# Head sums of a twelve-head attention over two streams instead of three: tiles 0 and 1 added before TensorE

## The chip, the core and the metric

One core of one Trainium2 chip runs the whole program. The metric is the time of one execution on the device, in microseconds (us). Three timed runs of the kernel before took 866.79, 868.4 and 868.53 us; their median is 868.4 us.

## The reference

The input `x` has 32 images of 384 channels and 32x32 = 1024 positions. Each image is normalised over 32 groups of channels, projected, passed through an attention that has no query and key but only statistics of one projection, projected again, and added to the input:

```python
w = einsum('bnc,oc->bno', gn(x), qkv_w)            # 12 heads of d = 32
norm = sqrt(sum(w * w, over positions))            # per channel
s = sum((w / max(norm, 1e-12))**2, over d)         # one score per head and position
Pi = softmax(s * temp, over the 12 heads)
Pi_n = Pi / (sum(Pi, over positions) + 1e-8)
dots = einsum('bhn,bhnd->bhd', Pi_n, w * w)
out = -(w * Pi) / (1 + dots)
y = x + einsum('bnc,oc->bno', out, out_w) + out_b
```

Everything is fp32. The score of a head is a sum over its 32 channels of `w * w`, each weighted by the channel's inverse squared norm and the head's `temp`.

## The kernel before

Channels lie on the 128 partitions in three tiles of [128, 1024] (t = 0, 1, 2), positions on the free axis; `W` of an image is written to the three PSUM tiles `acc[:, t]`. Each tile holds four heads; its 128 output channels are ordered so that the head is the fast index, and `PIB[:, t]` (the softmax weights of four heads, spread over 128 partitions through DRAM) matches that order.

Both projections are made in split fp32: each operand is a high part (`W1H`, `XH`, `W2H`, `UH`, rounded for the fast mode of TensorE) and a low remainder (`W1L`, `XL`, ...). A product of one output tile is 18 matmuls of 128x512: for each k of three, high by high and high by low weight (`n` = 0, 1), then the low operand (`n` = 2), each in two halves of 512 positions.

Images are software-pipelined, and the order on every engine is written out by hand as a function `step(i)`; steps 2 to 31 follow a prologue, and the loop over images 2 to 29 is unrolled four times. Engines meet at counting semaphores only. In step i:

- TensorE (PE) makes the first product of image i (three tiles, lines 824 to 826), then the second product of image i-1 (lines 827 to 830). Within tile 0 of the second product, before its first low term, `head_sums(i)` (line 789) runs: for each of three tiles and each quarter of the positions a matmul of the squares with `headsum[:, t]` (128x32), summed in `scores`. In the last step with an image (i = 31, `late`), they stand two matmuls earlier.
- ScalarE (ACT) squares each tile of `acc` into `WS` with a sum per channel into `sumsq` (`square_w`, line 501), copies `acc` into `WV` (`keep_w`, line 512), rounds the weighted `WV` of image i-1 to `UH` (`u_hi`, line 491), and makes `XN` and `XH` of image i+1 (lines 519, 529).
- VectorE (DVE) adds bias and input to the finished tiles (`finish`, line 1149), then, for image i-1, `dot` for three tiles (line 1041), four small steps of `attention`, `weigh` for three tiles (line 1067), and `u_lo`: `UL = WV - UH` (line 1141, two tiles before the group statistics, one after). `head_sum_weights(i)` (lines 990 to 996) makes `inv` and `headsum` from `sumsq` of all three tiles; softmax follows (lines 1005 to 1033).
- GpSimd (POOL) only makes `XL = XN - XH` for image i+1 (`x_lo`, line 424).
- SyncE (SP) loads, stores, and in `spread_pi` (line 366) writes `PIT` to DRAM in three DMAs and reads it back, broadcast, as three DMAs of 528 KB into `PIB`.

The prologue (image 0) and image 31 use other forms (`attend_tile`, `product_by_k`, heads of tile 0 spread by TensorE).

Of the kernel before, what the change touches and what calls it, by code (L numbers as in the profile page):

```python
# [33 lines left out]
P = 128  # L34
# [12 lines left out]
HEADSUM_STEPS = 3  # L47
IDLE_TURNS = (4, 4)
SM_SHIFTED, SM_STEPS = 3, 8
ATTENDED = 3 + 4  # L50
# [33 lines left out]
def conv_attention(nc, x, qkv_w, temp, out_w, out_b, y):  # L84
# [5 lines left out]
    HPT = P // D  # L90
    HALVES = N // BANK
# [8 lines left out]
    with ExitStack() as ctx:  # L100
# [46 lines left out]
        inv = sb("inv", [P, 2, T])  # L147
# [5 lines left out]
        pi_part = sb("pi_part", [P, HPT])  # L153
        pi_heads = sb("pi_heads", [P, BLOCKS, HPT])
        PIT = sb("PIT", [P, T, QUAD + 1])
        PIB = sb("PIB", [P, T, BLOCKS * QUADS, QUAD + 1])
# [13 lines left out]
        small = spread_ps[:, 0]  # L170
        temp_ps = scores[:, C:C + HEADS]
# [32 lines left out]
        headsum_step = sem("headsum_step")  # L204
        scores_done = sem("scores_done")
# [3 lines left out]
        pi_spread = [sem(f"pi_spread_{t}") for t in range(T)]  # L209
# [52 lines left out]
        def rows_moved(j, t, more=0):  # L262

            return j.counts(16, more - (16 if t == 0 and True else 0))
# [75 lines left out]
        def _(sp):  # L340
# [25 lines left out]
            def spread_pi(j):  # L366

                if has(j):
# [3 lines left out]
                    tiles = range(1 if by_pe(j) else 0, T)  # L372
                    for t in tiles:
                        rows = pi_dram[t * HPT:(t + 1) * HPT].rearrange("h (b q n) -> q (h b) n", b=BLOCKS, q=QUADS)
                        sp.dma_start(rows, PIT[:, t, :]).then_inc(pi_written[t], 16)
                    for t in tiles:
                        sp.wait_ge(pi_written[t], rows_moved(j, t, 16))
                        heads = pi_dram[t * HPT:(t + 1) * HPT].unsqueeze(0)\
                            .to_broadcast([D, HPT, BLOCKS * QUADS * (QUAD + 1)])
                        sp.dma_start(PIB[:, t].rearrange("p b n -> p (b n)"), heads).then_inc(pi_spread[t], 16)  # L380

# [26 lines left out]
        def _(pool):  # L408
# [7 lines left out]
            pool.tensor_copy(mixed_w2.rearrange("p (m d h) -> p m d h", d=D, h=HPT),  # L416
                             raw_w2.rearrange("p (m h d) -> p m d h", d=D, h=HPT)).then_inc(w2_mixed, 1)
# [8 lines left out]

            def step(i):
                for t in range(T):
                    x_lo(i + 1, t)
# [23 lines left out]
        def _(act):  # L453
# [83 lines left out]
            def widen_heads(j):  # L537

                act.wait_ge(heads_kept, pe_spread(j))
                if j.follows(1):  # L540
                    act.wait_ge(u_step, (j - 1).counts(U_STEPS, 1))
                act.activation(wide_heads(j).rearrange("p (b d h) -> p b d h", b=BLOCKS, d=D),
                               pi_heads[:].unsqueeze(2).to_broadcast([P, BLOCKS, D, HPT]), ACT.Copy)\
# [62 lines left out]
            def x_hi_first():  # L606
# [20 lines left out]
            act.activation(wide_part(last).rearrange("p (d h) -> p d h", d=D),  # L627
                           pi_part[:].unsqueeze(1).to_broadcast([P, D, HPT]), ACT.Copy).then_inc(heads_widened, 1)
# [14 lines left out]
        def _(pe):  # L643
            def turn_weights(ks):
# [3 lines left out]
                for k in ks:  # L648
                    for m in range(T):
                        raw = columns1[:, k, m, :] if k < T else columns2[:, k - T, m, :]  # L650
                        if k < T:
                            into = turned(k)[:, m * P:(m + 1) * P].rearrange("p (d h) -> p h d", h=HPT)
# [45 lines left out]
            def first_product(i, t):  # L698
# [6 lines left out]
                if has(i):  # L705
                    acc_left(i - 2, t)
                    product(acc[:, t, :], t, (W1H, W1L), (XH, XL), before, {}).then_inc(m1_done, 1)

# [80 lines left out]
            def head_sums(i):  # L789
# [7 lines left out]
                for t in range(T):  # L797
                    for q in range(QUADS):
                        block_q = square_tile(i, t).rearrange("p (b q r) -> p q b r", q=QUADS, r=QUAD)[:, q]
                        last = pe.matmul(scores[q * QUAD:(q + 1) * QUAD, 0:N // QUADS], headsum[:, t, :],  # L800
                                         block_q, start=(t == 0), stop=(t == T - 1))
# [17 lines left out]
            def step(i):  # L819
# [7 lines left out]
                second_product(i - 1, 0, {(1, 2) if late else (2, 0): lambda: head_sums(i)})  # L827

# [448 lines left out]
```

## Time and profile before

| what | before |
|---|---|
| timed runs | 866.79, 868.4, 868.53 us |
| profiled execution, first to last instruction | span 864.9 us |
| around the span (timed runs less span) | 1.9 to 3.6 us |
| PE busy | 851.6 us, 98% |
| DVE busy | 750.2 us, 87% |
| ACT busy | 528.3 us, 61% |
| POOL busy | 232.6 us, 27% |
| granted TensorE clock | 1.00 of full speed |

The profile is of one execution apart from the timed runs; its whole time is not given, only the span. Busy times are unions per engine. A line of the page's groups holds the line in the kernel, the engine, the operation, output and inputs, their shapes and count; then busy us and mean ns of one; then idle us in front of it and what ended them.

### The profile page before, as it was taken

What the parts mean: (1) busy time and instruction counts of PE and PEld (TensorE: products, weight loads), DVE (VectorE), ACT (ScalarE), POOL (GpSimd) and SP (SyncE); (2) the same over time, 40 slices, a digit from 0 to 9 for tenths busy, and PEclk for the clock granted to TensorE, in tenths of its full rate; (3) what the DMA queues carried; (4) which work ended last, traced back from release to release, by engine and by line L of the source; (5) the groups of instructions that cost most, each with busy time, mean ns of one, the idle gap of its engine ahead of it and who ended that gap; (6) DMA issues with size and microseconds to landing.
All of it is one profiled execution on the core that took longest, in us unless ns stands there. A gap on an engine that the chain in (4) does not pass through costs nothing.

```text
span 864.9 us, 14022 instructions
## 1 busy us (share of the span) xinstructions
PE 851.6 (98%) x4290; PEld 677.7 (78%) x4290; DVE 750.2 (87%) x1396; ACT 528.3 (61%) x680; POOL 232.6 (27%) x106
## 2 busy tenths in 40 slices
PE   7999999999999999999999999999999999999997
PEld 6767788777787777787777787777887777887776
DVE  7989889898888888888888898888898888898777
ACT  3567656567555677556676556676565675566642
POOL 2432123332123331133331233321233321233300
PEclk9999999999999999999999999999999999999999
DMA  7324665544664544664535654445655446645225
GB/s 279 119 79 153 225 229 185 185 148 169 225 227 161 197 146 181 226 223 160 180 150 198 228 213 168 163 145 220 227 186 196 141 163 225 228 175 186 88 86 197
DMA packets 45259, 157.42 MB, mean 182 GB/s; under 512 B 19866, under 2 KB 23962, under 8 KB 37274
## 3 DMA queue, kind: packets, MB, share of 16 engines
q1 hardware_dynamic: 36856, 154.10, 48.5%
q10 hardware_dynamic: 8354, 2.85, 1.3%
q14 instruction: 40, 0.33, 0.1%
q8 instruction: 9, 0.15, 0.1%
HBM read 104.47 MB, written 52.45 MB: 181 GB/s over the span
## 4 chain that ended last, share of the span: by engine, by line
PE 92%; DVE 4%; issue 1%; DMA 1%; ACT 1%; DVEq 0%; ACTq 0%
PE acc L678 86%; PE spread_ps L800 5%; DVE stats L906 1%; DVE WS L1041 1%; DMA PIB<-pi 0%; DMA X<-in_x 0%; DVE WV L1101 0%; DVE X L1149 0%; PE acc L655 0%; DVE WS L1080 0%; ACT WS L501 0%; DMA pi<-PIT 0%; DVE X L1116 0%; ACT WV L512 0%; PE spread_ps L815 0%
## 5 line engine op out<-in xcount | busy, mean ns | idle before, releaser
L424 POOL TENSOR_TENSOR XL<-XN,XH 128x1024 fp32r<-128x1024 f32 x93 | 222.9, 2414 | 571.7 <-ACT XH L529 548.2
L501 ACT ACTIVATE WS<-acc 128x1024 f32<-128x1024 f32 x96 | 98.4, 1026 | 240.5 <-PE acc L678 197.1
L678 PE MATMUL acc<-XH,W1H 128*128 128x512 f32 x574 | 177.3, 390 | 0.1
L678 PE MATMUL acc<-XH,W1L 128*128 128x512 f32 x574 | 176.8, 389 | 0.0
L678 PE MATMUL acc<-UH,W2H 128*128 128x512 f32 x558 | 172.6, 390 | 1.3 <-ACT WV L512 1.2
L678 PE MATMUL acc<-UH,W2L 128*128 128x512 f32 x558 | 172.3, 390 | 0.0
L678 PE MATMUL acc<-XL,W1H 128*128 128x512 f32 x576 | 146.2, 389 | 0.0
L678 PE MATMUL acc<-UL,W2H 128*128 128x512 f32 x558 | 145.3, 396 | 0.0
L1149 DVE SCALAR_TENSOR_TENSOR X<-acc,bias,X 128x1024 f32<-128x1024 f32 x93 | 116.3, 1276 | 31.0 <-PE acc L678 31.0
L678 PEld LDWEIGHTS acc<-UL,W2H 128*128 128x128 f32 x558 | 102.3, 188 | 32.2 <-issue 11.9
L678 PEld LDWEIGHTS acc<-XL,W1H 128*128 128x128 f32 x576 | 108.0, 188 | 22.7 <-POOL XL L434 0.3
L678 PEld LDWEIGHTS acc<-XH,W1L 128*128 128x128 f32 x574 | 107.7, 188 | 22.5
L678 PEld LDWEIGHTS acc<-XH,W1H 128*128 128x128 f32 x574 | 107.3, 188 | 23.0 <-issue 0.9
L678 PEld LDWEIGHTS acc<-UH,W2H 128*128 128x128 f32 x558 | 104.3, 188 | 24.9 <-issue 2.1
L1041 DVE CUSTOM_DVE_ANT_0 WS<-PIB,WS 128x1024 f32<-128x1024 f32 x94 | 113.5, 1222 | 10.2 <-DMA PIB<-pi 8.1
L906 DVE BATCH_NORM_STATS2 stats<-X 128x6 f32<-128x512 f32 x192 | 120.0, 680 | 2.5 <-DMA X<-in_x 2.5
L678 PEld LDWEIGHTS acc<-UH,W2L 128*128 128x128 f32 x558 | 104.6, 188 | 22.4 <-issue 0.4
L491 ACT ACTIVATE UH<-WV 128x1024 fp32r<-128x1024 f32 x93 | 95.0, 1054 | 41.7 <-DVE WV L1067 37.5
L519 ACT ACTIVATE XN<-X,norm 128x1024 f32<-128x1024 f32 x91 | 112.3, 1235 | 0.4 <-DVE XN L961 0.4
L1141 DVE TENSOR_TENSOR UL<-WV,UH 128x1024 fp32r<-128x1024 f32 x93 | 111.2, 1222 | 0.1
L1067 DVE SCALAR_TENSOR_TENSOR WV<-WV,dots,PIB 128x1024 f32<-128x1024 f32 x90 | 110.3, 1281 | 1.1
L529 ACT ACTIVATE XH<-X,norm 128x1024 fp32r<-128x1024 f32 x90 | 111.0, 1233 | 0.0
(119 smaller groups left out, 501.3 us busy)
## 6 DMA issues: line engine op xcount, KB each, us to landing
PIB<-pi SPq DMA_DIRECT2D x94, 528.0 KB, 5.1
X<-in_x SPq DMA_DIRECT2D x31, 1536.0 KB, 6.3
out_y<-X SPq DMA_DIRECT2D x30, 1536.0 KB, 6.5
gathered<-stats_rows ACTq DMA_DIRECT2D x28, 72.0 KB, 5.1
pi<-PIT SPq DMA_DIRECT2D x94, 16.5 KB
X<-in_x SPq DMA_DIRECT2D x3, 512.0 KB, 4.7
out_y<-X SPq DMA_DIRECT2D x1, 1024.0 KB, 6.0
out_y<-X SPq DMA_DIRECT2D x2, 512.0 KB, 2.6
```

Source lines behind the costliest of these rows:

```text
L424: pool.tensor_tensor(XL[:, t, :], XN[:, t, :], XH[:, t, :].bitcast(F32), ALU.subtract).then_inc(xl_done, 1)
L491: act.activation(u_tiles(j)[0][:, t, :], w_tile(j, t), ACT.Copy).then_inc(uh_done, 1)
L501: act.activation(square_tile(i, t), acc[:, t, :], ACT.Square, accum_out=sumsq[:, t:t + 1]).then_inc(squared, 1)
L519: act.activation(XN[:, t, :], x_tile(j, t), ACT.Identity, bias=shift_j, scale=rstd_j).then_inc(xn_done, 1)
L529: act.activation(XH[:, t, :], x_tile(j, t), ACT.Identity, bias=shift_j, scale=rstd_j).then_inc(xh_done, 1)
L678: last = pe.matmul(out[:, h * BANK:(h + 1) * BANK], w[:, k, m * P:(m + 1) * P], r[:, k, h * BANK:(h + 1) * BANK], start=(n == 0 and k == 0 ...
L800: last = pe.matmul(scores[q * QUAD:(q + 1) * QUAD, 0:N // QUADS], headsum[:, t, :], block_q, start=(t == 0), stop=(t == T - 1))
L906: last = dve.bn_stats(stats[:, k, :], X[:, j.slot, k * BANK:(k + 1) * BANK])
L1041: dve.tensor_tensor_reduce(in_blocks(square_tile(j, t)), PIB[:, t, :, 0:QUAD], in_blocks(square_tile(j, t)), 1.0, 0.0, ALU.mult, ALU.add, ...
L1067: dve.scalar_tensor_tensor(in_blocks(w_tile(j, t)), in_blocks(w_tile(j, t)), dots[:, 3, t:t + 1], PIB[:, t, :, 0:QUAD], ALU.mult, ALU.mult ...
L1141: dve.tensor_tensor(low[:, t, :], w_tile(j, t), high[:, t, :].bitcast(F32), ALU.subtract).then_inc(ul_done[t], 1)
L1149: dve.scalar_tensor_tensor(x_tile(j, t), acc[:, t, :], bias[:, t:t + 1], x_tile(j, t), ALU.add, ALU.add).then_inc(y_done, 1)
```

## The change

Tiles 0 and 1 get a common layout of eight heads by sixteen channels per head and tile, tile 2 keeps four heads by thirty-two. The channels of w that belong to one head of the first eight now lie half in tile 0 and half in tile 1, on the same partitions. So the squares of both tiles, each scaled by the channel's inverse squared norm, can be added elementwise, and one matmul stream with the constant `head_temp` serves both. From image 2 on:

- DVE: `pair_weight(i, t)` makes the inverse squared norms of tiles 0 and 1 as soon as each is squared; `head_sum_weights` handles tile 2 only, with its inverse in PSUM; `u_lo` leaves the engine.
- ACT: `scale_square` scales the squares of tile 0 (after `keep_w(i, 0)`) and of tile 1 (after the last `u_hi`).
- POOL: `u_lo` of tile 0, the addition of the scaled squares, `u_lo` of tiles 1 and 2, then `x_lo`.
- PE: `head_sums` has two streams; of the second product the high terms of tile 0 come first, then the head sums, the high terms of tile 1, the low terms of tiles 0 and 1, and tile 2. The late step keeps its order.
- `PIB` has two bands instead of three tiles: three writes to DRAM, then two broadcast reads of 528 KB. Images 0 and 31 write all three parts too.

```diff
+        paired = sb("paired", [P, 2, N])
-        PIB = sb("PIB", [P, T, BLOCKS * QUADS, QUAD + 1])
+        PIB = sb("PIB", [P, BANDS, BLOCKS * QUADS, QUAD + 1])
+        inv_ps = small[:, QUAD:QUAD + 2 * T].rearrange("p (s t) -> p s t", t=T)
...
 # SyncE, spread_pi
+                    for band, of_band in enumerate(BAND_HEADS):
+                        for t in range(of_band.start // HPT, of_band.stop // HPT):
+                            sp.wait_ge(pi_written[t], j.counts(16, 16))
...
 # GpSimd
+            def u_lo(j, t):
+                pool.wait_ge(uh_done, j.counts(T, t + 1))
+                wait_weighed(pool, j, T - 1)
+                pool.wait_ge(m2_done, j.counts(T))
+                pool.tensor_tensor(UL[:, t, :], w_tile(j, t), UH[:, t, :].bitcast(F32),
+                                   ALU.subtract).then_inc(ul_done[t], 1)
             def step(i):
+                if i.follows(2) and has(i):
+                    u_lo(i - 1, 0)
+                    pool.wait_ge(pair_step, i.counts(PAIR_STEPS, 2 - PAIR_STEPS * PAIRED))
+                    pool.tensor_tensor(paired[:, 0, :], paired[:, 0, :], paired[:, 1, :], ALU.add).then_inc(pair_step, 1)
+                    u_lo(i - 1, 1)
+                    u_lo(i - 1, 2)
                 for t in range(T):
                     x_lo(i + 1, t)
...
 # ScalarE
+            def scale_square(i, t):
+                if has(i):
+                    act.wait_ge(headsum_step, i.counts(HEADSUM_STEPS, 2 * t + 2))
+                    act.wait_ge(squared, i.counts(T, t + 1))
+                    act.wait_ge(scores_done, i.counts(1))
+                    act.activation(paired[:, t, :], square_tile(i, t), ACT.Copy, scale=inv[:, 1, t:t + 1]).then_inc(pair_step, 1)
             def step(i):
                 square_w(i, 0)
                 keep_w(i, 0)
+                scale_square(i, 0)
                 u_hi(i - 1, 0)
                 square_w(i, 1)
                 u_hi(i - 1, 1)
                 u_hi(i - 1, 2)
+                scale_square(i, 1)
                 square_w(i, 2)
...
 # TensorE, head_sums
+                if paired_sums(i):
+                    pe.wait_ge(pair_step, i.counts(PAIR_STEPS, PAIR_STEPS - PAIR_STEPS * PAIRED))
+                    streams = [(head_temp[:, 0, :], paired[:, 0, :]), (headsum[:, T - 1, :], square_tile(i, T - 1))]
 # TensorE, step
+                second_high(i - 1, 0)
+                head_sums(i)
+                second_high(i - 1, 1)
+                second_low(i - 1, 0)
+                second_low(i - 1, 1)
+                second_high(i - 1, 2)
+                second_low(i - 1, 2)
...
 # VectorE
+            def pair_weight(j, t):
+                link = chain(headsum_step, j.counts(HEADSUM_STEPS, 2 * t))
+                dve.wait_ge(squared, j.counts(T, t + 1))
+                dve.wait_ge(scores_done, j.counts(1))
+                link(dve.tensor_scalar(inv[:, 0, t:t + 1], sumsq[:, t:t + 1], NORM_FLOOR ** 2, None, ALU.max))
+                link(dve.reciprocal(inv[:, 1, t:t + 1], inv[:, 0, t:t + 1]), follows=False)
 # attention, step 0: two sums in place of one
+                    dve.tensor_reduce(total[:, 0:2], PIB[:, 0, :, QUAD].unsqueeze(1).to_broadcast([P, 2, BLOCKS * QUADS]),
+                                      AX_X, ALU.add).then_inc(u_step, 1)
+                    done = dve.tensor_reduce(total[:, 2:3], PIB[:, 1, :, QUAD], AX_X, ALU.add)
             def step(i):
+                pair_weight(i, 0)
                 weigh(i - 1, 0)
                 weigh(i - 1, 1)
                 weigh(i - 1, 2)
-                u_lo(i - 1, 0)
-                u_lo(i - 1, 1)
+                pair_weight(i, 1)
                 group_moments(i + 1)
                 head_sum_weights(i)
                 group_norm(i + 1)
-                u_lo(i - 1, 2)
                 group_stats(i + 2, [0])
                 softmax_shift(i)
```

## Rows read from the trace of the kernel before

**Rows 1.** The page's first part: TensorE's busy time, share of the span, instructions.
```profile
PE 851.6 (98%) x4290; PEld 677.7 (78%) x4290; DVE 750.2 (87%) x1396; ACT 528.3 (61%) x680; POOL 232.6 (27%) x106
```
**Rows 2.** Chain that ended last, one step of 28: start, us, what.
```profile
416.72 1.43 PE spread_ps L800 x24
418.15 24.72 PE acc L678 x108
```
**Rows 3.** Timeline of TensorE, one step: start, us, engine, line, operation.
```profile
401.60 0.62 PE L678 MATMUL acc<-XH,W1H 128*128 128x512 f32 x2
...
413.84 0.62 PE L678 MATMUL acc<-UH,W2H 128*128 128x512 f32 x2
...
427.75 0.62 PE L678 MATMUL acc<-XH,W1H 128*128 128x512 f32 x2
```
**Rows 4.** Timeline of VectorE and ScalarE, same step; in brackets idle time before.
```profile
404.19 1.23 DVE L1041 CUSTOM_DVE_ANT_0 WS<-PIB,WS 128x1024 f32<-128x1024 f32 x1
...
405.59 1.23 DVE L1041 CUSTOM_DVE_ANT_0 WS<-PIB,WS 128x1024 f32<-128x1024 f32 x1 [0.17 <-DMA PIB<-pi]
...
407.71 3.68 DVE L1067 SCALAR_TENSOR_TENSOR WV<-WV,dots,PIB 128x1024 f32<-128x1024 f32 x3
...
409.03 1.06 ACT L491 ACTIVATE UH<-WV 128x1024 fp32r<-128x1024 f32 x1 [0.96 <-DVE WV L1067]
...
410.11 1.03 ACT L501 ACTIVATE WS<-acc 128x1024 f32<-128x1024 f32 x1
...
411.13 2.00 ACT L491 ACTIVATE UH<-WV 128x1024 fp32r<-128x1024 f32 x2
...
414.19 1.03 ACT L501 ACTIVATE WS<-acc 128x1024 f32<-128x1024 f32 x1 [1.07 <-PE acc L678]
...
415.34 0.17 DVE L990 TENSOR_SCALAR inv<-sumsq 128x3 f32<-128x3 f32 x1 [0.96 <-ACT WS L501]
```
**Rows 5.** Page, DMA issues: count, KB each, us to landing.
```profile
PIB<-pi SPq DMA_DIRECT2D x94, 528.0 KB, 5.1
```
**Rows 6.** Timeline of ScalarE and GpSimd: waking after an XH; three subtractions in a row.
```profile
418.62 1.24 ACT L529 ACTIVATE XH<-X,norm 128x1024 fp32r<-128x1024 f32 x1
...
419.99 2.40 POOL L424 TENSOR_TENSOR XL<-XN,XH 128x1024 fp32r<-128x1024 f32 x1 [18.28 <-ACT XH L529]
...
812.09 7.20 POOL L424 TENSOR_TENSOR XL<-XN,XH 128x1024 fp32r<-128x1024 f32 x3 [18.08 <-ACT XH L529]
```
**Rows 7.** Groups by shape: busy us, mean ns of one, idle before.
```profile
L491 ACT ACTIVATE UH<-WV 128x1024 fp32r<-128x1024 f32 x93 | 95.0, 1054 | 41.7 <-DVE WV L1067 37.5 <-DVE WV L1101 4.2
...
L519 ACT ACTIVATE XN<-X,norm 128x1024 f32<-128x1024 f32 x91 | 112.3, 1235 | 0.4 <-DVE XN L961 0.4
...
L450 POOL TENSOR_TENSOR X<-XN,X 128x512 f32<-128x512 f32 x1 | 1.3, 1273 | 40.6 <-ACT XN L637 40.6
```
**Rows 8.** Timeline near the end: ScalarE ends, TensorE resumes after a wait.
```profile
852.18 1.06 ACT L491 ACTIVATE XH<-WV 128x1024 fp32r<-128x1024 f32 x1 [2.11 <-DVE WV L1101]
...
853.29 0.72 PE L678 MATMUL acc<-XH,W2H 128*128 128x512 f32 x2
853.85 0.63 PE L678 MATMUL acc<-XH,W2L 128*128 128x512 f32 x2
```
**Rows 9.** Timeline of the first step with two streams (69 to 88 us) and the late one.
```profile
69.28 3.68 DVE L1067 SCALAR_TENSOR_TENSOR WV<-WV,dots,PIB 128x1024 f32<-128x1024 f32 x3
...
87.76 0.61 PE L678 MATMUL acc<-XH,W1H 128*128 128x512 f32 x2
...
820.05 0.61 PE L678 MATMUL acc<-XH,W1H 128*128 128x512 f32 x2
...
836.65 1.55 PE L678 MATMUL acc<-UL,W2H 128*128 128x512 f32 x6
```
**Rows 10.** Timeline of the prologue: a small VectorE instruction beside a GpSimd subtraction.
```profile
21.70 2.97 POOL L438 TENSOR_TENSOR W2L<-WV,W2H 128x384 fp32r<-128x384 f32 x3
...
23.96 0.27 DVE L924 TENSOR_SCALAR spread<-offset,part_mv 128x1 f32<-128x1 f32 x1
```

More of the change, by code:

```diff
@@ L260, in pe_spread, with band_rows, paired_sums @@
             return 2 if j.follows(1) else 1
-        def rows_moved(j, t, more=0):
-            return j.counts(16, more - (16 if t == 0 and True else 0))
+        def band_rows(t):
+            return PIB[:, BAND[t], :, 0:QUAD]
+        def paired_sums(j):
+            return j.follows(PAIRED)
         def tile_steps(j, t, steps):
@@ L651, in turn_weights @@
                         if k < T:
-                            into = turned(k)[:, m * P:(m + 1) * P].rearrange("p (d h) -> p h d", h=HPT)
+                            band = BAND_HEADS[m * HPT // PAIR_HEADS]
+                            heads = slice(m * HPT - band.start, (m + 1) * HPT - band.start)
+                            into = turned(k)[:, band.start * D:band.stop * D].rearrange("p (d h) -> p h d", h=len(band))[:, heads]
                         else:
@@ L707, in first_product, with second_high, second_low @@
                     product(acc[:, t, :], t, (W1H, W1L), (XH, XL), before, {}).then_inc(m1_done, 1)
+            def second_high(j, t):
+                pe.wait_ge(squared, (j + 1).counts(T, t + 1))
+                pe.wait_ge(w_kept, (j + 1).counts(T, t + 1))
+                for k in range(T):
+                    if t == 0:
+                        pe.wait_ge(uh_done, j.counts(T, k + 1))
+                    for n in (0, 1):
+                        term(acc[:, t, :], t, (W2H, W2L), (UH, UL), n, k)
+            def second_low(j, t):
+                for k in range(T):
+                    if t == 0:
+                        pe.wait_ge(ul_done[k], j.counts(1, 1))
+                    last = term(acc[:, t, :], t, (W2H, W2L), (UH, UL), 2, k)
+                last.then_inc(m2_done, 1)
             def second_product(j, t, inside):
@@ L987, in head_sum_weights @@
                     return
-                link = chain(headsum_step, j.counts(HEADSUM_STEPS))
+                tiles = slice(T - 1, T) if paired_sums(j) else slice(0, T)
+                done = 4 if paired_sums(j) else 0
+                link = chain(headsum_step, j.counts(HEADSUM_STEPS, done))
                 dve.wait_ge(squared, j.counts(T, T))
-                link(dve.tensor_scalar(inv[:, 0, :], sumsq[:], NORM_FLOOR ** 2, None, ALU.max))
-                link(dve.reciprocal(inv[:, 1, :], inv[:, 0, :]))
+                link(dve.tensor_scalar(inv_ps[:, 0, tiles], sumsq[:, tiles], NORM_FLOOR ** 2, None, ALU.max))
+                link(dve.reciprocal(inv_ps[:, 1, tiles], inv_ps[:, 0, tiles]))
                 if j.follows(1):
@@ L995, in head_sum_weights @@
                     dve.wait_ge(temp_kept, 3)
-                link(dve.tensor_tensor(headsum[:], head_temp[:],
-                                       inv[:, 1, :].unsqueeze(2).to_broadcast([P, T, QUAD]), ALU.mult), follows=False)
+                weights = headsum[:, tiles, :]
+                dve.tensor_tensor(weights, head_temp[:, tiles, :], inv_ps[:, 1, tiles].unsqueeze(2).to_broadcast(weights.shape),
+                                  ALU.mult).then_inc(headsum_step, HEADSUM_STEPS - 2 - done)
+            def pair_weight(j, t):
+                if not has(j):
+                    return
+                link = chain(headsum_step, j.counts(HEADSUM_STEPS, 2 * t))
[3 more added lines that the diff above has]
+                link(dve.reciprocal(inv[:, 1, t:t + 1], inv[:, 0, t:t + 1]), follows=False)
             def softmax_shift(j):
@@ L1029, in softmax_divide @@
                     for t in range(T):
-                        if j.follows(2) or rows_moved(j, t) > 0:
-                            dve.wait_ge(pi_written[t], rows_moved(j, t))
+                        dve.wait_ge(pi_written[t], j.counts(16))
                 link(dve.transpose(PIT[:, :, 0:QUAD], scores[:, P:P + HEADS * BLOCKS]))
```

106 lines of the change are left out of this document (58 added, 48 removed).

## The prediction

> **What bounds the kernel now.** I read the busy shares first: TensorE is busy for 851.6 of 864.9 us, all other engines have idle time [rows 1]. The chain of waits agrees: step after step it is TensorE alone, 24.72 us of product matmuls and 1.43 us of head sums, together 26.15 us [rows 2]. The timeline gives the same period: step 3 begins at 87.76 and step 31 at 820.05, so 28 steps take 732.29 us, 26.15 each [rows 9]. What a step of TensorE loses is thus worth 28 times as much, but only as long as no other engine's chain becomes longer than the step. The reader should see in the timeline of one step how near that is: ScalarE's third square waited 1.07 us for TensorE [rows 4], and GpSimd was idle for some 18 us of each step before its first subtraction [rows 6]. So the question is whether the new work fits into these gaps in its order, not whether the engines have the time in total.
>
> All times below are those of the step that begins at 401.60 [rows 3]. Its 54 matmuls up to 413.84 give one per 0.2267 us [rows 3]. The sum is made as a difference to the profiled execution (span 864.9 us) and then put on the median, 868.4 us; what lies around the span, 1.9 to 3.6 us, I leave as it is.
>
> **Part 1, what goes.** One of three streams of head sums leaves TensorE: 1.43/3 = 0.48 us [rows 2]. If nothing else changed, a step would take 25.67 us. Bounds: 0 (if the passes were limited by something other than the streamed columns) to 0.48. I take 0.48. Three `u_lo` leave VectorE, which was no bound; and one of three broadcasts of 528 KB goes [rows 5]. The third `dot` waited for one, 405.59 instead of a start some 0.2 us earlier [rows 4]. I take that wait as gone, since softmax also comes no later than before and less is moved; if it stays, 0.2 us come back below.
>
> **Part 2, the new chain.** The head sums now need both scaled squares and their sum, and the low terms of tile 0 need three `UL` that GpSimd makes around this sum. I follow the chain.
>
> VectorE: before `weigh` there are three small instructions more (the second sum of `attention`, two of `pair_weight`). None is longer than 0.20 us, the size of L990 with its gap [rows 4]; the independent ones overlap with their neighbours. I take 0.33 us in all, bounds 0.2 and 0.6. `weigh` moves from 407.71 to 407.71 - 0.21 + 0.33 = 407.83. `u_hi` of tile 0 followed `weigh` by 1.32 us [rows 4], now 409.15. The scaling of the first square fits in front of it: ScalarE was idle there for 0.96 us [rows 4] and the scaling takes about as long. The square of tile 1 started at 410.11, when TensorE had finished that tile (36 matmuls of 0.2267 = 8.16 us after 401.60, and the wake); it stays there within 0.06 us.
>
> ScalarE: two `u_hi` from 411.13 take 2.00 us; as two of 1.054 [rows 7] in 2.00 [rows 4] overlap by 0.11, the next one begins at 413.02. That is the second scaling. No row has a copy with one factor per partition. A plain copy from SBUF takes 1.054, one with factor and offset per partition 1.235 [rows 7]; I take the middle, 1.14. It ends at 414.16, and the third square, at 414.19 [rows 4], is just not delayed. So ScalarE's old gap hides it; if the cover were 0.1 us shorter, that would move the third square, on which nothing here hangs, as the path now goes through GpSimd.
>
> GpSimd: `u_lo` of tile 0 follows the third `weigh` (407.83 + 3.68 = 411.51 [rows 4]) and takes 2.41, done by 414.05. The addition wakes 0.13 us after ScalarE's end, as the subtraction at 419.99 did after 418.62 + 1.24 [rows 6]: 414.29. Three operations in a row take 7.20 us [rows 6]. For the addition, fp32 out, the nearest row is 1.273 us for half the size [rows 7]; doubled, 2.55, is its upper bound, as the fixed part counts twice, and 2.40 like the subtraction is my value. The sum is there at 414.29 + 2.40 = 416.69, the third `UL` at 421.49.
>
> TensorE: it is ready for the head sums at 416.65 [rows 2], so their wait costs 0.1 to 0.2 us. Then 0.95 us of head sums, 12 high and 4 low matmuls take it to about 421.4 without that wait (25.67 - 26 x 0.2267 = 19.78 after 401.60: 421.38). The third `UL` comes at 421.49; TensorE resumes 0.05 us after a release and its first pair takes 0.11 us more than a pair in stream (852.18 + 1.06 to 853.29; 0.56 to the next pair instead of 0.453) [rows 8]. So the low terms of k = 2 count from 421.65, and the last 26 matmuls end 5.89 us later, at 427.54 instead of 427.75 [rows 3]. **A step gains 0.21 us, not 0.48**, and its bound is now the chain through GpSimd; the first wait of head sums is inside it. 28 steps: -5.9 us.
>
> **Part 3, the two ends.** In step 2 VectorE was late: `weigh` began at 69.28, and the next step at 87.76 [rows 9]. No `dot` waited there, so `weigh` moves by 0.33 to 69.61, and the chain from it to the next step is 427.54 - 407.83 = 19.71 us: 89.32, 1.6 us later than before. In step 31 the order is the old one: only 14 matmuls stand between TensorE's beginning of the head sums and the low term of k = 2, while GpSimd needs two `u_lo` of 2.40 after the addition. That term began at 836.65 + 4 x 0.2267 = 837.56; now at 820.05 + 20.05 = 840.10 [rows 9]. What follows, the spreading of the last image's heads and its tail, hangs on TensorE's order behind it, so 2.5 us come on. Bounds for both ends together: 0 (if the tail has slack that I don't see) to 4.1; I take 4.1. The prologue's changes (one more 16.5 KB write, two copies of the weights instead of one, eight heads instead of four in two small products) I cost at nothing, 0.5 us if a `dot` there waits.
>
> **Sum.** -5.9 + 1.6 + 2.5 = -1.8: 866.6 us. A measurement of this kernel tells about 0.2%, 1.7 us, from no change, so the forecast lies at the edge of that.
>
> **Rivals.** (A) TensorE stays the bound. If GpSimd's chain were 0.27 us shorter, the step is 25.67: -13.4 us, and the ends +3.5: 858.5. For it: the scaling could cost the plain 1.054, the DVE chain could be quicker by the whole `dot` wait. Against: each of these gives 0.1. Times between 858.5 and 864 belong here.
>
> (B) The chain is dearer: scaling 1.235 (+0.10) and addition 2.55 (+0.15) make the step 26.19: +1.1, ends +4.6: 874. Slower from the point where the step passes 26.0 us, because then the ends are no longer paid for. With 0.6 us for VectorE's small instructions, another 0.3 us a step, over 880. For it: each of the values has a row at that end. Against: they would have to be dear together.
>
> (C) VectorE and GpSimd block each other. At 411.5 `pair_weight` of tile 1 (a maximum, then a reciprocal that follows 0.2 us later) meets the start of `u_lo` of tile 0. If the reciprocal had to stay behind the subtraction until 414.0, the second scaling would begin 1.2 us late, and so would all behind it: 28 x (1.2 - 0.2) and ends of 6.6: about 903. It decides if the reciprocal starts after GpSimd. Against it: in the prologue a one-element instruction of VectorE ran at 23.96 in 0.27 us within GpSimd's subtractions from 21.70 to 24.67 [rows 10], so it did not sit one out. The Trainium skill ("SBUF — State Buffer", section "SBUF: two separate sides") says that VectorE and GpSimd share a pair of ports as an exclusive lock for a whole instruction, taken by VectorE's operations in a two-port mode or with two SBUF inputs. By that rule the reciprocal could be locked out, and `dot` and `weigh` would have to keep clear of GpSimd's subtractions; the row at 23.96 shows no such wait for one element, and no run here shows the two-input case.
>
> (D) The head sums do not shrink (the four quarters share the array, and no row shows two streams): the step stays at 26.15 and the ends cost about 4: 872.
>
> **Chances.** Forecast 0.53, with times from 863.8 (gain 0.31 a step) to 869.4 (0.11), half of it on either side of 866.7: 0.26 faster, 0.27 same. A 0.19, faster. B 0.15, C 0.08, D 0.05, slower. Together 0.45 faster, 0.27 same, 0.28 slower. Range 860 to 875: it leaves out the best of A, the worst of B, and C. The likeliest case alone: 863.8 to 869.4.
>
> **What would show it.** In the timeline after: a step of 25.9 us; head sums of 0.95 us; TensorE idle for one or two tenths in front of the head sums and again before the low term of k = 2 of tile 0, released by GpSimd's `UL`; the chain of waits running through GpSimd and ScalarE instead of TensorE alone; the second scaling at 11.4 us into a step and 1.14 us long; 2.5 us of waiting in the late step. TensorE without idle and a step of 25.67 would be A; a reciprocal of `pair_weight` that starts when a subtraction ends would be C; head sums of 1.43 us, D. The forecast is wrong if the step is under 25.8 or over 26.1 us.

## The result, and the profile after

| | before | after |
|---|---|---|
| timed runs, median | 868.13 us (7, 866.79 to 869.46) | 870.62 us (7, 868.5 to 874.07) |
| ratio after / before, 95% interval | | 1.0037 [1.0026, 1.0047] |
| profiled execution, span | 864.9 us | 866.7 us (whole time 868.5) |
| step 3 begins, step 31 begins | 87.76, 820.05 | 89.39, 819.34 |
| mean of 28 steps | 26.15 us | 26.07 us |
| TensorE busy | 851.6 us | 842.8 us |

The kernel became slower by 0.37%, where the point forecast was 0.2% faster. The busy shares alone would suggest the contrary: TensorE is busy for 8.8 us less than in [rows 1].

The page's first part, after (engine, busy us, share, instructions):

```profile
PE 842.8 (97%) x4050; PEld 667.0 (77%) x4050; DVE 664.7 (77%) x1456; ACT 584.1 (67%) x740; POOL 515.8 (60%) x227
```

The waits of after that bear on the chain (who waited, for what: us in total, times, longest us; PEld is TensorE's weight load):

```profile
PEld spread_ps L867 <- POOL paired L457: 20.0, 28, 2.7
PEld acc L722 <- POOL UL L450: 8.5, 30, 2.0
DVE WS L1128 <- DMA PIB<-pi: 3.7, 13, 0.4
```

TensorE waits in front of the head sums for GpSimd's sum and before the low term for `UL`, the two places that the prediction named. The 20.0 and 8.5 us are idle time of the weight loads, and not what the matmuls lose: the head sums start 15.33 us into a step in the mean, where they started at 15.05 before, so 0.28 us a step where 0.1 to 0.2 was forecast. Here is the step from 402.76 to 428.74, which answers to [rows 3, 4]. The timelines of VectorE, ScalarE, GpSimd and TensorE (start, us, engine, line, operation):

```profile
404.34 1.23 DVE L1128 CUSTOM_DVE_ANT_0 WS<-PIB,WS 128x1024 f32<-128x1024 f32 x1
...
409.15 3.68 DVE L1156 SCALAR_TENSOR_TENSOR WV<-WV,dots,PIB 128x1024 f32<-128x1024 f32 x3
...
410.47 1.06 ACT L523 ACTIVATE UH<-WV 128x1024 fp32r<-128x1024 f32 x1
...
414.33 1.14 ACT L584 ACTIVATE paired<-WS,inv 128x1024 f32<-128x1024 f32 x1
415.37 1.01 ACT L533 ACTIVATE WS<-acc 128x1024 f32<-128x1024 f32 x1
...
412.91 2.41 POOL L450 TENSOR_TENSOR UL<-WV,UH 128x1024 fp32r<-128x1024 f32 x1 [9.14 <-DVE WV L1156]
415.54 2.40 POOL L457 TENSOR_TENSOR paired<-paired 128x1024 f32<-128x1024 f32 x1 [0.23 <-ACT paired L584]
417.90 4.78 POOL L450 TENSOR_TENSOR UL<-WV,UH 128x1024 fp32r<-128x1024 f32 x2
...
418.00 0.64 PE L867 MATMUL spread_ps<-paired,head_temp 128*32 128x256 f32 x8
418.46 0.61 PE L867 MATMUL spread_ps<-WS,headsum 128*32 128x256 f32 x8
```

Every link of the predicted chain is there with its predicted length: the scaling 1.14, the addition 2.40, head sums of 1.00 us (418.00 to 419.00), released by GpSimd. But the chain begins late. The first `dot` starts 1.58 us into this step; in all 28 steps of before a first `dot` starts at 1.40, right behind the finish of the last tile. After, it does so in three steps of 28, with 1.64 as the mean and 1.88 as the worst. Where it starts at 1.40, the step takes 25.80 to 25.83 us (428.74 to 454.57, say): shorter than forecast.

What the late `dot` waits for stands in the chain of waits of after, in one of the steps where the chain leaves TensorE (start, us, what):

```profile
759.73 0.26 ACT spread_ps L567
...
761.16 0.26 DVE PIT L1120
...
761.44 0.57 SPq L388
...
762.07 2.09 DMA pi<-PIT
...
764.24 4.86 DMA PIB<-pi
...
769.12 0.07 DVE WS L1128
```

From ScalarE's exponentials through softmax, the write to DRAM and the broadcast it takes 9.4 us, and the `dot` begins when the broadcast lands. Band 0 needs two writes to land before it can be read, where a tile needed one. SyncE's timeline shows the price, before (first two lines) and after, in the step of the rows above:

```profile
422.31 1.72 SPq L375 DMA_DIRECT2D pi<-PIT  x3
424.46 1.88 SPq L380 DMA_DIRECT2D PIB<-pi  x3
```

```profile
422.62 1.80 SPq L388 DMA_DIRECT2D pi<-PIT  x3
425.50 1.22 SPq L394 DMA_DIRECT2D PIB<-pi  x2
```

From the first write's issue to the broadcast's issue: 2.15 us before (mean of steps 3 to 30, none over 2.17), 2.82 after.

That is one of two lengths that grew. The first broadcast also lands later after its own issue, 4.78 us in the mean instead of 4.10. For the two that are issued at 424.46 and 425.50 the trace gives, before and after:

```profile
DMA to landing us min/median/max: 4.2/4.2/4.2
```

```profile
DMA to landing us min/median/max: 4.6/4.6/4.6
```

Against these 0.67 and 0.68 us softmax comes earlier: the first write is issued 0.57 us earlier, seen from the step that needs it. In all, the first broadcast lands 0.78 us into that step before and 1.56 after (means of steps 3 to 30). Before, it was there 0.6 us ahead of the `dot`; after, the `dot` waits for it. Why this broadcast takes longer no run shows.

### The profile page after: what moved, and what is told of

It reads as the page before. It is cut to its first block and busy times, and to the rows that moved or that the text cites. A ratio compares the mean times of both kernels' runs of the same rounds, so it can differ in the third digit from the quotient of the medians.

```text
span 866.7 us, 14147 instructions
## 1 busy us (share of the span) xinstructions
PE 842.8 (97%) x4050; PEld 667.0 (77%) x4050; DVE 664.7 (77%) x1456; ACT 584.1 (67%) x740; POOL 515.8 (60%) x227
## 3 DMA queue, kind: packets, MB, share of 16 engines
q10 hardware_dynamic: 8354, 2.85, 1.3%
## 5 line engine op out<-in xcount | busy, mean ns | idle before, releaser
L450 POOL TENSOR_TENSOR UL<-WV,UH 128x1024 fp32r<-128x1024 f32 x90 | 215.0, 2403 | 276.9 <-DVE WV L1156 276.9
L722 PE MATMUL acc<-UH,W2H 128*128 128x512 f32 x558 | 176.0, 397 | 1.7 <-ACT WV L544 1.2
L722 PE MATMUL acc<-UL,W2H 128*128 128x512 f32 x558 | 139.7, 394 | 1.6 <-POOL UL L450 1.6
L722 PEld LDWEIGHTS acc<-UH,W2H 128*128 128x128 f32 x558 | 102.0, 188 | 35.1 <-issue 14.0
L1128 DVE CUSTOM_DVE_ANT_0 WS<-PIB,WS 128x1024 f32<-128x1024 f32 x94 | 110.4, 1222 | 4.7 <-DMA PIB<-pi 3.7
```

Source lines behind the costliest of these rows:

```text
L450: pool.tensor_tensor(UL[:, t, :], w_tile(j, t), UH[:, t, :].bitcast(F32), ALU.subtract).then_inc(ul_done[t], 1)
L722: last = pe.matmul(out[:, h * BANK:(h + 1) * BANK], w[:, k, m * P:(m + 1) * P], r[:, k, h * BANK:(h + 1) * BANK], start=(n == 0 and k == 0 ...
L1128: dve.tensor_tensor_reduce(in_blocks(square_tile(j, t)), band_rows(t), in_blocks(square_tile(j, t)), 1.0, 0.0, ALU.mult, ALU.add, dots[:, ...
```

## The experiments

Theory 1: the late first `dot` makes the step. Up to e6 I took it as a chain (dot, weigh, GpSimd, head sums); e5 showed that it is a loop through two images, and e7 to e9 test that. The third square cannot start before TensorE has its tile (12.59 us into the step). From the square on, ScalarE's queue, exponentials, softmax, writes and broadcast take 15.0 us to the next `dot` (180.49 to 195.51 in the trace of after). With a step of 26.15 such a `dot` would be due at 12.59 + 15.02 - 26.15 = 1.46, almost hidden behind the finish; with 25.83 it is due at 1.78. With the 0.67 us less of one write it would be due at 0.79 and 1.11, hidden both times. This takes the square at its earliest; in the trace of after it starts at 12.73 in the mean, up to 13.03, since a late `dot` makes ScalarE's queue in front of the square late. Rivals: shared ports of VectorE and GpSimd hold the `dot`; ScalarE's two new scalings push the exponentials; the whole loss lies in the late step. Steps are means over steps 3 to 30. Ratios are to the kernel before, timed beside each run.

| run | us, median | ratio, 95% | mean step |
|---|---|---|---|
| e1_softmax_first | 867.35 | 0.9996 [0.9986, 1.0006] | 25.99 |
| e2_band1_first | 882.34 | 1.0184 [1.0164, 1.0204] | 26.45 |
| e3_inv_sbuf | 885.02 | 1.0206 [1.0192, 1.0220] | 26.58 |
| e4_late_order | 869.7 | 1.0028 [1.0017, 1.0038] | 26.09 |
| e5_scale_earlier | 868.12 | 1.0003 [0.9993, 1.0013] | 26.07 |
| e6_step2_turns | 871.07 | 1.0043 [1.0030, 1.0056] | 26.03 |
| e7_exp_first | 868.3 | 1.0011 [1.0002, 1.0020] | 26.02 |
| e8_one_scaling | 863.99 | 0.9961 [0.9948, 0.9975] | 25.89 |
| e9_one_write_less | 862.31 | 0.9942 [0.9928, 0.9955] | 25.85 |
| v1_slack | 897.88 | 1.0346 [1.0327, 1.0364] | 27.10 |
| v2_slack_old_order | 905.96 | 1.0439 [1.0421, 1.0457] | 27.36 |
| v3_three_orders | 861.37 | 0.9928 [0.9914, 0.9941] | 25.86 |

**e1, softmax and exponentials earlier.**

```diff
-                group_stats(i + 2, [0])
                 softmax_shift(i)
                 softmax_divide(i)
-                group_stats(i + 2, range(1, T))
+                group_stats(i + 2, range(T))
 # ScalarE
                 normalise(i + 1, 0)
-                x_hi(i + 1, 0)
                 exponentials(i)
+                x_hi(i + 1, 0)
```

> Only the order changes: VectorE makes the whole softmax of an image before the next statistics, ScalarE its exponentials one operation earlier. Theory 1 (softmax loop): in the changed kernel most steps lose 0.1 to 0.5 us because the first dot waits for the first broadcast of the softmax weights, which lands some 7.5 us after PIT is done; then PIT is done 0.7 to 1 us earlier here, every first dot starts 1.40 us into its step, the step falls from a mean of 26.07 to 25.82 us and the time by 7 us, from 870.6 to 863.6. Theory 2 (ports): the first dot, with two SBUF inputs, is held by GpSimd's last subtraction; then the dots stay as late as before and the time stays at 870.6.

Measured: as fast as the kernel before, so the loss is gone, but not the 0.4% hoped for. Of 28 first dots 21 start at 1.40, and those steps take 25.78 to 25.95. The other seven, every fourth step, take 26.07 to 26.63. There the writes come out of the queue later; SyncE in a common step and in such a one:

```profile
188.06 1.68 SPq L388 DMA_DIRECT2D pi<-PIT  x3
190.83 1.22 SPq L394 DMA_DIRECT2D PIB<-pi  x2
...
213.71 1.73 SPq L388 DMA_DIRECT2D pi<-PIT  x3
217.57 1.22 SPq L394 DMA_DIRECT2D PIB<-pi  x2
```

3.86 us instead of 2.77 between the two issues. So the way through softmax holds the `dot`, and a shorter way frees it; the ports don't.

**e2, band 1 written, broadcast and used first.** The writes go in the order 2, 0, 1, band 1 is broadcast ahead of band 0, and VectorE's dots follow that order (ScalarE's waits on single dots become waits for all three).

```diff
...
-                for t in range(T):
+                for t in (2, 0, 1):
                     dot(i - 1, t)
...
```

> Softmax stays where it is, but tile 2, which needs one write only, is written, broadcast and dotted first, tiles 0 and 1 behind it. Theory 1: the first dot starts at 1.40 us again, as one write of 16.5 KB less lies in front of its broadcast; the second may wait up to 0.5 us for the later band; 864 to 867. Theory 2: unchanged, 870.6, as GpSimd's work is the same.

Measured: slower by 1.8%. The first `dot` starts at 1.40 as wanted, but the second waits for band 0, whose broadcast now lies behind the other's 528 KB:

```profile
435.06 1.22 DVE L1129 CUSTOM_DVE_ANT_0 WS<-PIB,WS 128x1024 f32<-128x1024 f32 x1
436.80 1.23 DVE L1129 CUSTOM_DVE_ANT_0 WS<-PIB,WS 128x1024 f32<-128x1024 f32 x1 [0.51 <-DMA PIB<-pi]
```

It came at 2.54 to 3.86 us into the step. The wait was moved and grew; this bears on the transfers as the cause, not on their size. ScalarE's changed waits are in this run too (its second square starts at 9.16 in the mean, after at 8.77), and their share of the loss isn't told apart.

**e3, inverse norms in SBUF.**

```diff
-        inv = sb("inv", [P, 2, 2])
+        inv = sb("inv", [P, 2, T])
-        inv_ps = small[:, QUAD:QUAD + 2 * T].rearrange("p (s t) -> p s t", t=T)
+        inv_ps = inv[:]
```

> One part undone: the inverse norms of tile 2 lie in SBUF instead of PSUM, so the product that makes its head weights has two SBUF inputs while GpSimd adds the squares. If VectorE and GpSimd exclude each other for whole instructions, the product waits for the end of the addition (about 0.9 us after its present start) and the head sums start 0.3 us or more later in each step: 879 or more. If they do not: the three small instructions stay at their places and the time at 870.6.

Measured: slower by 2.1%. VectorE's small product for the head sums (0.19 us after) takes 1.09; VectorE, then GpSimd:

```profile
424.31 0.15 DVE L1067 TENSOR_SCALAR inv<-sumsq 128x1 f32<-128x1 f32 x1 [2.64 <-ACT WS L533]
424.50 0.16 DVE L1068 RECIPROCAL inv<-inv 128x1 f32<-128x1 f32 x1
424.70 1.09 DVE L1074 TENSOR_TENSOR headsum<-head_temp,inv 128x32 f32<-128x32 f32 x1
```

```profile
423.36 2.38 POOL L457 TENSOR_TENSOR paired<-paired 128x1024 f32<-128x1024 f32 x1 [0.22 <-ACT paired L584]
425.69 2.39 POOL L450 TENSOR_TENSOR UL<-WV,UH 128x1024 fp32r<-128x1024 f32 x1
```

It ends when the addition has ended; the two instructions ahead of it, with one SBUF input each, take 0.15 and 0.16 us beside the same addition. That is the lock that rival C spoke of, for an instruction with two SBUF inputs; the rule of the Trainium skill ("SBUF — State Buffer", section "SBUF: two separate sides") agrees with the trace in this. With the norms in PSUM the change avoids it. Softmax follows the longer wait, so the first dots come still later (2.02 in the mean).

**e4, the late step in the normal order.**

```diff
-                if late:
-                    second_product(i - 1, 0, {(1, 2): lambda: head_sums(i)})
...
                 second_low(i - 1, 0)
+                if late:
+                    spread_heads(i)
                 second_low(i - 1, 1)
+                if late:
+                    spread_totals(i)
```

> Only step 31 changes: its low terms of tile 0 come after the high terms of tile 1, as in the other steps, with the spreading of the last heads behind them. If the late step costs the 2.5 us that the prediction worked out, the time falls from 870.6 to 868.1 and the tail from the start of step 31 is as long as in the kernel before or shorter (44.85 us); if the tail is bound by VectorE and its transfers, it stays at 47.4 us and the time at 870.6.

Measured: from step 31 to the end 45.9 us, against 47.36 after and 44.85 before: 1.5 of the 2.5 us come back; where the other 1.0 comes from no run shows. The time's interval overlaps that of after: the late step is a part of the loss, not its core.

**e5, the second scaling one place earlier.**

```diff
                 u_hi(i - 1, 1)
-                u_hi(i - 1, 2)
                 scale_square(i, 1)
+                u_hi(i - 1, 2)
                 square_w(i, 2)
```

> ScalarE makes the scaled square of tile 1 one place earlier: before UH of tile 2 instead of after it. Theory 1 (the step is set by the chain dot, weigh, GpSimd, head sums): the scaling then starts about 0.9 us earlier and is no longer what the addition waits for; the addition starts when UL of tile 0 leaves GpSimd, some 0.2 us earlier than before (10.2 + 2.4 = 12.6 us into the step instead of 12.83), and the step goes from 26.07 to about 25.87: 28 x 0.2 = 5.6 us off the changed kernel, about 865 us. Theory 2 (the order on ScalarE matters more than the wake: UH of tile 2 or the square of tile 2 comes later and TensorE waits there instead): the step stays at 26.0 to 26.2, 869 to 873 us.

Measured: the scaling does come 0.95 us earlier, counted from the first `dot` (it starts 10.54 to 11.42 us into the step, 11.34 to 11.99 after), and the addition then starts as soon as `UL` of tile 0 is made, but the mean step stays 26.07. The first dots have become later, 1.93 in the mean and none at 1.40. This is what a loop does: the head sums come earlier, TensorE's step would end earlier, and the way through softmax, which is no shorter, is late by as much. The third square, at 13.00 in the mean, starts later still than after. Theory 1 as it stands in this expectation, a chain, was wrong. The median lies 2.5 us below that of after; of this the profiled executions show 0.6 (step 2 takes 28.58 us instead of 29.02, the end 47.15 instead of 47.33), and the rest stays open.

**e6, filling TensorE's wait in step 2.** In the traces of e1, e2, e7 and e9 the granted clock is 0.51 to 0.58 from 79.7 to 83.1 us, its lower level of 1.2 GHz, behind the head sums of step 2, for which TensorE had just waited 2.3 us; in those of after and e4 it stays at 1.00, 2.4 GHz, behind waits of 2.24 and 2.28 us. The windows of e1 (busy time and number for each engine, granted clock, DMA share, GB/s):

```profile
55.00:79.60 24.60, 21.80 (x106) 16.48 (x104) 19.69 (x37) 14.40 (x20) 10.51 (x5) 1.00 0.52 179
79.60:83.10 3.50, 3.50 (x12) 2.80 (x9) 2.59 (x9) 3.23 (x4) 3.50 (x2) 0.51 0.00 0
```

Where it happens, step 3 begins at 90.8 to 91.0 instead of 89.3 to 89.4: 1.5 us. That was the reason for the run. The wait of 2.3 us is not the only place: e3's trace has the lower level from 80.5 us behind 2.53 us and again from 855.4, v3's from 78.6 behind two waits of 0.8 us, and v2's, at 186.7 and 514.3, in the midst of its steps.

```diff
                 if paired_sums(i):
+                    if not i.follows(3):
+                        idle_turns(scores[:, 0:P], 9)
                     pe.wait_ge(pair_step, i.counts(PAIR_STEPS, PAIR_STEPS - PAIR_STEPS * PAIRED))
...
```

> TensorE's first four steps are written out ahead of its loop, and in step 2 nine multiplications of a matrix of ones fill the 2.2 us that it waits before the head sums. Theory 1 (in some executions the granted clock falls to half for 3.5 us behind this wait, as at 79.6 to 83.1 us in e1's trace, and that costs 1.5 us): with the wait filled no execution shows it; step 2 takes 29.0 us (up to 29.2 if the turns overrun), and the median goes from about 870.3 to about 869. Theory 2 (the dips have nothing to do with the wait): spans and granted clocks of the runs stay spread as they are (0.995 to 0.999), median within 0.5 us of the changed kernel.

Measured: inconclusive. I had put the turns behind another wait of the head sums, so that 1.48 us of idle time stayed, and they then ran 2.27 us, 1.5 longer than the wait; step 3 begins at 90.85 with the clock at 1.00. The lower level comes in this trace all the same, from 839.4 us in the late step. How much of the timed runs' distance to the profiled execution the clock explains stays open.

**e7, the exponentials' place alone** (ScalarE's half of e1's diff).

> ScalarE's exponentials go ahead of XH of tile 0; nothing else is moved. Theory 1 (the first dot is late because of what lies between the third square and it: ScalarE's queue up to the exponentials, softmax, three writes, the broadcast; in the changed kernel 15.0 us from the square to the next dot, so that with a step of 25.83 the dot would start 12.59 + 15.02 - 25.83 = 1.78 us into the step): exponentials come 0.5 us earlier (they then wait for softmax's shift), the dot would be due at 1.3 and starts at 1.40, where the finish lets it; most steps take 25.83, the sum falls by up to 28 x 0.24 = 6.7 us, some less for the loop turns: 865 to 867 us. Theory 2 (the gain of e1 came from softmax ahead of the statistics): no change, 870 us.

Measured: 23 of 28 steps do what was expected (25.82 to 25.95), and 21 dots start at 1.40. The other five take 26.25 to 27.34, and so the mean is 26.02. In the worst of them the broadcast lands 6.1 us after its issue and the `dot` waits 1.37 us for it; e1 has its late steps at the same distance of four. The time was 1.3 us above the expected upper end.

**e8, without the second scaling.**

```diff
-                    act.activation(paired[:, t, :], square_tile(i, t), ACT.Copy, scale=inv[:, 1, t:t + 1]).then_inc(pair_step, 1)
+                    columns = slice(0, N) if t == 0 else slice(0, 1)
+                    act.activation(paired[:, t, columns], square_tile(i, t)[:, columns], ACT.Copy,
+                                   scale=inv[:, 1, t:t + 1]).then_inc(pair_step, 1)
 # GpSimd adds square_tile(i, 1) in place of paired[:, 1, :]
```

> ScalarE scales only one column of tile 1's square; GpSimd adds the unscaled square instead. Left out: the factor of tile 1. ScalarE has 0.95 us less per step ahead of the third square. Theory 1 (the dot is late by the second write of band 0 and the shorter step; ScalarE's scaling isn't what makes it late, for the third square can't start before TensorE's product is ready at 12.59 anyway): the first dots stay late, 1.6 to 1.9 us into the step; the addition starts when UL of tile 0 is made, and what is gained there (0.1 to 0.2) the dot gives back: step 25.9 to 26.05, 866 to 870 us. Theory 2 (the scalings on ScalarE's queue push the exponentials and so the dot): the dot comes 0.95 us earlier, at 1.40 in all steps, and the step is 25.7 to 25.8: 860 to 863 us.

Measured: the mean step is 25.89, the dots stay late (1.68 in the mean, eight of 28 at 1.40 to 1.42). So the second scaling isn't what delays the dots, and theory 2 falls on that; the first one stayed in. The third squares all start by 12.60 here (12.59 in the mean), so ScalarE's queue is not needed for late dots. But the time fell below theory 1's, as the addition now waits for nothing but `UL` of tile 0. Here one late `dot`, and GpSimd without a gap in front of the addition:

```profile
194.51 1.23 DVE L1130 CUSTOM_DVE_ANT_0 WS<-PIB,WS 128x1024 f32<-128x1024 f32 x1 [0.51 <-DMA PIB<-pi]
```

```profile
203.07 2.40 POOL L450 TENSOR_TENSOR UL<-WV,UH 128x1024 fp32r<-128x1024 f32 x1 [9.52 <-DVE WV L1158]
205.42 2.40 POOL L457 TENSOR_TENSOR paired<-paired,WS 128x1024 f32<-128x1024 f32 x1
```

**e9, one write for band 0.**

```diff
-                    for t in range(T):
+                    for t in (0, 2) if j.follows(2) else range(T):
                         rows = pi_dram...
-                        for t in range(of_band.start // HPT, of_band.stop // HPT):
+                        for t in (2 * band,) if j.follows(2) else range(of_band.start // HPT, of_band.stop // HPT):
                             sp.wait_ge(pi_written[t], j.counts(16, 16))
...
 # VectorE waits for the same writes alone before it makes PIT again
```

> From the third image on tile 1's weights of attention aren't written, and band 0's broadcast waits for tile 0's write alone. Left out: the fresh weights of tile 1's heads (those of the second image stay). Theory 1 (second write): from the first write's issue to the broadcasts' issue it takes 2.15 us instead of 2.78, the first dot is due at 1.15 and starts at 1.40 in nearly all steps; step 25.83, 28 x 0.24 = 6.7 us less: 864 us. Theory 2 (ScalarE's queue alone): dots stay late by 0.1 to 0.3 us, 868 us or more.

Measured: the two issues of SyncE lie 2.14 us apart in the mean, as before the change, and in no step over 2.16:

```profile
421.00 1.14 SPq L388 DMA_DIRECT2D pi<-PIT  x2
423.16 1.22 SPq L394 DMA_DIRECT2D PIB<-pi  x2
```

All 28 first dots start at 1.40 (one at 1.41), the mean step is 25.85, and the kernel, else unchanged, is 0.6% faster than before. Taking out the second write is thus enough to turn the loss into a gain; this run decided it. e8 and e9 are alike up to the first write (issued at 19.90 and 19.89 us into the step) and differ from there by the second one: band 0 lands 1.57 and 0.89 us into the next step. The slower landing of the broadcast stays in e9 (4.70 us). Had it stayed at the 4.10 of before, the same sum puts the landing of after at 0.88, in time as well; no run tries that.

**v1 and v2, more slack for the head sums.** Both have e4's order, e5's order, GpSimd's addition ahead of `u_lo(i - 1, 0)`, and TensorE's `second_high(i - 1, 2)` ahead of the low terms of tile 0; v1 has e1's orders too.

> The changed kernel with five orders changed: softmax ahead of the statistics and exponentials one place earlier (as in e1), the late step in the normal order (as in e4), the scaling of tile 1 before UH of tile 2, GpSimd's addition before UL of tile 0, and TensorE's high terms of product tile 2 before the low terms of tile 0, so that UL may come 2.8 us later. Theory 1 (chain through dot, scaling and addition sets the step): the addition starts at about 11.7 us into the step and ends 0.9 us before TensorE is through its high terms (14.97), both waits of TensorE go, and the step is TensorE's own, 25.83 less 0.12 before the head sums and about 0.1 before the low term: 25.6. From the changed kernel 28 x 0.45 = 12.6 and 1.5 of the late step: about 856 us. Theory 2 (another wait takes their place, at the third square, the head sum weights or the low terms): the step stays at 25.8 or above, 862 us or more.

> As v1, but softmax and exponentials stay where the changed kernel has them. Theory 1 (the first dot comes late by 0.1 to 0.5 us, and costs time only because nothing between it and the head sums has slack): the 0.9 us of slack that v1 has takes it up; step 25.6 to 25.65, within 1.5 us of v1. Theory 2 (late dots cost TensorE elsewhere too, through w and UH): 0.1 to 0.2 more per step than v1, 3 to 6 us.

Measured: both much slower. The three finishes now come back to back, and GpSimd, which starts its row of seven instructions with the addition instead of filling the time in front of it, is through with `XL` 3.2 us into the next step instead of 1.05. In 22 of the 28 steps the first `dot` of v1 meets it, VectorE, then GpSimd:

```profile
252.50 2.85 DVE L1129 CUSTOM_DVE_ANT_0 WS<-PIB,WS 128x1024 f32<-128x1024 f32 x1
...
255.27 1.22 DVE L1129 CUSTOM_DVE_ANT_0 WS<-PIB,WS 128x1024 f32<-128x1024 f32 x1
```

```profile
247.12 7.14 POOL L442 TENSOR_TENSOR XL<-XN,XH 128x1024 fp32r<-128x1024 f32 x3
```

The `dot`, with two inputs from SBUF, takes 2.85 us instead of 1.22 and ends about one of its own lengths after GpSimd's last subtraction (247.12 + 7.14 = 254.26). The lengths fit e3's lock, now with a large instruction. These 22 steps take 26.65 us in the mean, and in v2, whose dots start later, 26.60. The other six, at distance four, take 28.73 in v1 and 30.15 in v2, and v2's 0.26 us a step more lies there. In them VectorE stands idle in front of the third finish (3.83 us before 172.77 in v1) and waits for nothing that the profile shows; the cause is open.

**v3, the orders of e1, e4 and e5 together.**

> The orders of e1, e4 and e5 together: softmax and exponentials earlier, the late step in the normal order, the scaling of tile 1 ahead of UH of tile 2. Theory 1 (two limits in turn: the first dot by the way through softmax, which e1 shortens, and the addition by ScalarE's scaling, which e5 shortens, so that each alone shows little): dots at 1.40 in three steps of four; the addition starts when UL of tile 0 is made (9.96 + 2.41 = 12.37), the head sums at 14.8 to 15.0, where TensorE itself is through its high terms; steps of 25.7, at the loop's turn 26.0: mean 25.8. From the changed kernel 28 x 0.27 = 7.6 and 1.5 of the late step: about 861.5 us, faster than both kernels. Theory 2 (TensorE's own wait takes their place): 865 us or more.

Measured: 861.37 us, 0.7% faster than the kernel before. 21 of 28 steps take 25.74 or 25.75, the seven at distance four 26.12 to 26.28. The step's rows show the addition following `UL` without a gap, and 15.05 us after the step's begin the head sums without a wait:

```profile
204.00 2.41 POOL L450 TENSOR_TENSOR UL<-WV,UH 128x1024 fp32r<-128x1024 f32 x1 [9.14 <-DVE WV L1155]
206.36 2.40 POOL L457 TENSOR_TENSOR paired<-paired 128x1024 f32<-128x1024 f32 x1
...
209.08 0.64 PE L867 MATMUL spread_ps<-paired,head_temp 128*32 128x256 f32 x8
```

In these 21 steps TensorE doesn't wait for the head sums, and the step is 0.40 us shorter than before, of the 0.48 that Part 1 put at most. But for the rest, the seven steps and the ends this is rival A's case, reached with three orders changed.

## Why the prediction was wrong

- **The step that failed** is Part 1's on the `dot`: "I take that wait as gone, since softmax also comes no later than before and less is moved". The third `dot`'s wait did go: neither it nor the second waits in any of the 28 steps. The first one got a wait in its place. Softmax did come earlier (0.57 us, seen from the step that needs it), but the first band takes two writes (2.82 us from issue to issue instead of 2.15) and its broadcast lands 4.78 us after its issue instead of 4.10, so that it lands at 1.56 instead of 0.78, behind the 1.40 at which the `dot` could start. I had counted the instructions and bytes of the changed DMAs and not what their first reader waits for. It costs 0.24 us a step (1.64 instead of 1.40), 28 x 0.24 = 6.7 us. e9 shows it by taking the second write out, e1 and v3 by making softmax earlier.
- **The third square.** Part 2 says of a later third square that "nothing here hangs" on it. Softmax, and with it the next step's first `dot`, hangs on it: after, it starts at 12.73 in the mean instead of 12.59, up to 13.03.
- **The chain of Part 2** was right in its links and a little too long in its sum: with the `dot` in time a step takes 25.80 to 25.83 and not 25.94, so it would have gained 0.33 us and not 0.21. Scaling 1.14 and addition 2.40 are as put; two `UL` in a row take 4.74 to 4.78 instead of 4.80, and from head sums to the next step it is 10.71 to 10.77 us.
- **Together** the two made 26.07: a gain of 0.08 a step in place of 0.21, 2.3 us instead of 5.9. That is the whole error of the sum for the profiled execution.
- **Part 3** was right: step 2 ends 1.63 us later (forecast 1.6), step 31 to the end takes 2.51 us longer (2.5), with TensorE waiting 1.58 us for the third `UL` there, at 838.93. So -2.3 + 1.6 + 2.5 = +1.8, which is 866.7 - 864.9.
- **The rest of the measured 2.5 us**, 0.7, is in executions other than the profiled one, which was the fastest of after at a granted clock of 1.00. The other six have mean clocks of 0.995 to 0.999, and e1's windows show a place where the clock falls. That this explains it is not shown: two of the six, at 0.999, were 1.5 and 2.1 us longer too.
- **Rivals.** B came nearest in size (a step that gains too little to pay for the ends), but by another mechanism. C didn't happen in the change: `pair_weight`'s reciprocal took 0.17 us beside GpSimd. With the norms in SBUF there is a wait of that kind, for the two-input product and not for the reciprocal (e3). D is refuted by head sums of 1.00 us in the place of 1.43. A was within reach (v3).

## What to carry to other kernels

When a change shortens the engine that bounds a pipelined loop, list every path from one turn to the next, with its length, and compare each with the new, shorter turn: here a broadcast that had landed 0.6 us ahead of its reader came 0.8 us later and was the bound afterwards. When parts of a transfer are merged, ask what its first reader waits for now, not how many bytes are saved. If two paths bound a step in turn, undoing either alone shows little (e1, e5), and the runs must be tried together (v3).

## What the runs showed of the hardware

- A VectorE instruction with two SBUF inputs ended late when GpSimd's elementwise instruction ran beside it: 1.09 instead of 0.19 us (e3) and 2.85 instead of 1.22 (v1). Instructions of one element per partition with one SBUF input didn't (0.15, 0.16).
- In some executions the granted clock fell to its lower level in step 2, for some 3.5 us (0.51 in e1), behind a wait of TensorE of 2.3 us (e1, e2, e7, e9) or two of 0.8 us (v3); in others, behind waits of 2.24 and 2.28 us, it stayed at 1.00 (after, e4), and so it did behind two of 0.8 us in e5.
- The first broadcast of 528 KB landed 4.10 us after its issue before the change and 4.70 to 4.78 us in after, e8 and e9 (means). The cause is open.
- Every fourth step (the loop's turn) the broadcast of that step was issued or landed some 1.1 to 1.3 us late in e1, e7 and v3 at the worst. One or two packets of the queue "instruction" stand in the DMA view of the late steps that I looked at, but one in that of a common step too; e9 had no late dots. The cause is open and was not tried.
